# Cross-attention on one core: softmax denominators by transposed sums on VectorE instead of matrix products with ones

## The reference, cut to what matters

```
a = layer_norm(ctx) * gamma + beta                  # (32, 375, 512)
Q = x @ Wq.T;  K = a @ Wk.T;  V = a @ Wv.T          # 16 heads of 32
attn = softmax(where(mask, Q K^T * 32**-0.5, -inf)) # over the 375 context rows
out = x + tanh(gate) * ((attn @ V) @ Wo.T)
```

## Time and profile before

| | |
|---|---|
| median of 3 runs | 940.44 us |
| the profiled execution, whole | 940.45 us |
| its span, first to last instruction | 938.4 us |
| PE busy | 928.2 us (99%) |
| DVE, ACT, POOL busy | 706.4, 685.8, 639.4 us |
| L1123, 992 records in the loop | 35.1 us busy, 259 ns each |
| L870, L873, L876, 31 each | 645, 241, 645 ns each |
| L855, 384 records | 625 ns each |
| L680, 62 records | 543 ns each |

### The profile page before, as it was taken

One profiled execution on the slowest core, in us unless ns is written; L12 is line 12 of the kernel. 1 busy time (PEld: TensorE's weight loads), 2 busy tenths in 40 slices (PEclk: granted clock), 3 DMA queues, 4 the chain that ended last, 5 costly groups with the idle time before them and its releaser, 6 DMA issues.

```text
span 938.4 us, 26747 instructions
## 1 busy us (share of the span) xinstructions
PE 928.2 (99%) x10723; PEld 805.9 (86%) x10723; DVE 706.4 (75%) x1381; ACT 685.8 (73%) x1296; POOL 639.4 (68%) x724
## 2 busy tenths in 40 slices
PE   9999999999999999999999999999999999999997
PEld 8898888888888888888888888888888888888885
DVE  6972498778777778777877777877787777887677
ACT  3422687777778787787877778777787777878775
POOL 0672366777777777777777777877777777777765
PEclk9999999999999999999999999999999999999999
DMA  9983143334344433444434443344443443334212
GB/s 280 344 266 150 29 101 93 92 104 115 90 98 113 111 92 88 104 113 116 105 85 111 115 107 82 93 111 114 115 98 90 113 114 95 91 94 113 56 39 59
DMA packets 85850, 105.54 MB, mean 112 GB/s; under 512 B 22528, under 2 KB 63488, under 8 KB 85728
## 3 DMA queue, kind: packets, MB, share of 16 engines
q1 hardware_dynamic: 85152, 102.93, 41.3%
q10 hardware_dynamic: 576, 0.92, 0.3%
HBM read 86.39 MB, written 17.43 MB: 111 GB/s over the span
## 4 chain that ended last, share of the span: by engine, by line
PE 95%; DMA 1%; DVE 1%; ACT 1%; SPq 0%; issue 0%; DVEq 0%
PE banks L959 66%; PE banks L1104 10%; PE banks L1117 8%; PE banks L982 7%; PE banks L1123 2%; DMA shared_f<-in_xT 1%; ACT shared_q L630 0%; ACT shared_q L639 0%; DMA x_odd<-row_stats 0%; DVE shared_q L865 0%; PE banks L1085 0%; DVE shared_r L751 0%; PE banks L990 0%; SPq L319 0%; ACT shared_f L644 0%
## 5 line engine op out<-in xcount | busy, mean ns | idle before, releaser
L959 PE MATMUL banks<-shared_r,w_k 128*128 128x376 f32 x1536 | 291.7, 339 | 0.6 <-ACT shared_f L680 0.5
L630 ACT ACTIVATE shared_q<-banks,maskT,rstd 125x448 f32<-125x448 f32 x384 | 243.4, 729 | 55.3 <-PE banks L1104 55.0
L959 PE MATMUL banks<-w_v,shared_r 128*125 128x512 f32 x1152 | 283.5, 395 | 0.0
L855 DVE TRANSPOSE_TENSOR_REDUCE rmax<-shared_q 128x14 f32<-128x448 f32 x384 | 219.8, 625 | 82.3 <-ACT shared_q L630 81.1
L959 PEld LDWEIGHTS banks<-shared_r,w_k 128*128 128x128 f32 x1536 | 263.1, 188 | 13.5 <-issue 0.9
L493 POOL TENSOR_TENSOR shared_f<-shared_q 125x448 f32<-125x448 f32 x124 | 142.0, 1145 | 163.7 <-PE banks L1123 163.2
L959 PEld LDWEIGHTS banks<-w_v,shared_r 128*125 128x125 f32 x1152 | 212.9, 186 | 44.5
L865 DVE TENSOR_TENSOR shared_q<-shared_q,banks 125x448 f32<-125x448 f32 x384 | 208.2, 607 | 0.1
L639 ACT ACTIVATE shared_q<-shared_q 125x448 f32<-125x448 f32 x384 | 186.4, 568 | 2.5 <-DVE shared_q L865 2.5
L497 POOL TENSOR_TENSOR shared_f<-shared_f,shared_q 125x448 f32<-125x448 f32 x124 | 142.3, 1148 | 9.7
L461 POOL TENSOR_TENSOR shared_r<-cn,shared_r 128x375 fp32r<-128x375 f32 x124 | 112.3, 927 | 42.9 <-ACT shared_r L591 42.8
(11 more groups left out here) (93 smaller groups left out, 785.1 us busy)
## 6 DMA issues: line engine op xcount, KB each, us to landing
cn<-in_ctxT SPq DMA_DIRECT2D x128, 187.5 KB, 4.0
rows<-in_ctx SPq DMA_DIRECT2D x32, 720.0 KB
xy<-in_x SPq DMA_DIRECT2D x32, 224.0 KB, 7.4
q_kept<-shared_q SPq DMA_DIRECT2D x8, 896.0 KB, 7.5
shared_q<-q_kept SPq DMA_DIRECT2D x32, 224.0 KB, 3.9
out<-xy SPq DMA_DIRECT2D x32, 224.0 KB, 3.8
shared_f<-in_xT SPq DMA_DIRECT2D x7, 896.0 KB, 11.3
x<-row_stats SPq DMA_DIRECT2D x64, 84.0 KB
```

The source lines that it names most:

```text
L630: act.activation(prob[0:SP_, n % NB, j, :] .rearrange("p (a h t) -> p a h t", a=2, h=2), score_view(n, j), ACT.Identity, bias=maskT[0:SP_, ...
L855: last = dve.tensor_reduce(rmax[:, n % 2, BLK * j:BLK * j + BLK], prob[:, n % NB, j, :].rearrange("p (k a) -> p k a", a=32), AX.X, ALU.max ...
L959: last = pe.matmul(dst, l, m, start=(start and k == 0), stop=(stop and k == len(pairs) - 1))
```

## The change

For batches 0 to 28 (SUMMED = B - 3 = 29, so slots p < 116) TensorE's products with ones are gone. VectorE takes a transposed sum of each `psum` half (`partial_sums`: one value per query and quadrant into `parts`). Once per batch SyncE stores these to DRAM and loads them so that the four quadrants lie side by side on 32 partitions (`store_parts`, `load_parts`); VectorE adds the four, takes the reciprocal and transposes (`shares`); SyncE stores the result and loads it back spread over all 128 partitions in four loads (`store_shares`, `load_shares`) into `rshare`. GpSimd multiplies with that one batch step later: `normalised(c-3)`, `add_bias(c-3)` and `low_half(c-3)` now all stand in the even slot pair, and ScalarE's `high_half(c-3)` in the middle of it. Batches 29 and 30 keep the way of before, and 31 the one that it has in the last steps. `psum`'s rows 96 to 127 are set to zero once, since the transposed sum reads all 128. GpSimd's `sum_chunks` waits for VectorE's sum of the buffer instead of TensorE's product.

```diff
+        SUMMED = B - 3
             for m in range(PAIRS):
                 c, odd = divmod(m, 2)
+                if summed(c - 2):
+                    if odd:
+                        store_shares(c - 2)
+                    else:
+                        store_parts(c - 2)
                 store_maxima(2 * m)
                 store_maxima(2 * m + 1)
                 load_maxima(2 * m)
                 load_maxima(2 * m + 1)
+                if summed(c - 2):
+                    if odd:
+                        load_shares(c - 2)
+                    else:
+                        load_parts(c - 2)
...
             def normalised(b):
-                pool.wait_ge(rspread_done, b + 1)
                 o = pv[:, b % 2 * HT:b % 2 * HT + HT]
-                pool.tensor_tensor(o, o, rspread[:, :], ALU.mult).then_inc(o_norm, 1)
+                if b < SUMMED:
+                    pool.wait_ge(ld_shares, 64 * b + 64)
+                    pool.wait_ge(pv_out, b * KT + KT)
+                    pool.tensor_tensor(o, o, rshare[:, :], ALU.mult).then_inc(o_norm, 1)
+                else:
+                    pool.wait_ge(rspread_done, b - SUMMED + 1)
+                    pool.tensor_tensor(o, o, rspread[:, :], ALU.mult).then_inc(o_norm, 1)
...
-                need(pool, pv_mm, p - 1)
+                if p - 2 < SUMMED * KT:
+                    need(pool, part_done, p - 1)
+                else:
+                    pool.wait_ge(pv_mm, p - 1)
...
-                if odd and 1 < c < B - 1:
-                    low_half(c - 2)
                 if not odd and m >= 0:
-                    if c > 1:
-                        normalised(c - 2)
+                    if c > 2:
+                        normalised(c - 3)
+                        add_bias(c - 3)
+                        low_half(c - 3)
+                    if m == PAIRS - 2:
+                        normalised(B - 3)
                     if c + 1 < B and c > 0:
                         row_statistics(c + 1)
-                    if c > 2:
-                        add_bias(c - 3)
...
+                if p < SUMMED * KT:
+                    act.wait_ge(sum_done, p + 2)
+                    at = p % 8 * T
+                    act.activation(pv[:, at:at + 2 * T], bank[b][:, 0:2 * T], ACT.Copy) \
+                        .then_inc(pv_out, 2)
+                    return
...
+            def partial_sums(p):
+                dve.wait_ge(sum_done, p + 1)
+                if p % KT == 0:
+                    need(dve, parts_stored, p // KT * 16)
+                u = p % KT
+                dve.tensor_reduce(parts[:, BLK * u:BLK * u + BLK],
+                                  psum[:, p % 2, :].rearrange("p (k a) -> p k a", a=32),
+                                  AX.X, ALU.add, apply_transpose=True).then_inc(part_done, 1)
+
+            def shares(b):
+                dve.wait_ge(ld_parts, 16 * b + 16)
+                n = KT * BLK
+                dve.tensor_reduce(whole_sum[:, 0:n], part4[:, :].rearrange("p (q k) -> p k q", q=HC),
+                                  AX.X, ALU.add).then_inc(whole_done, 1)
+                dve.wait_ge(whole_done, b + 1)
+                dve.reciprocal(whole_sum[:, 0:n], whole_sum[:, 0:n]).then_inc(share_step, 1)
+                dve.wait_ge(share_step, b + 2)
+                need(dve, shares_stored, 16 * b)
+                dve.transpose(share_rows[:, :], whole_sum[:, :]).then_inc(share_done, 1)
...
-                if not odd and c > 1:
-                    normalise(c - 2)
+                if m == PAIRS - 2:
+                    normalise(B - 3)
...
+                for p in (2 * m - 4, 2 * m - 3):
+                    if 0 <= p < SUMMED * KT:
+                        partial_sums(p)
+                if not odd and 0 <= c - 2 < SUMMED:
+                    shares(c - 2)
...
+                if p < SUMMED * KT:
+                    last.then_inc(pv_mm, 2)
+                    return
                 for q in range(2):
                     pe.wait_ge(sum_done, p + q + 1)
                     denominator(psum[:, q, :], to[:, (2 + q) * T:(3 + q) * T], True, True) \
```

More of the change, by code:

```diff
@@ L544, in _ @@
                 pool.memset(prob[96:128, q, :, :], LOWEST).then_inc(low_done, 1)
-            pool.wait_ge(low_done, NB)
             pool.wait_ge(q_out, GROUPS * KT)
+            for q in range(2):
+                pool.memset(psum[96:128, q, :], 0.0).then_inc(low_done, 1)
+            pool.wait_ge(low_done, NB + 2)
             pool.wait_ge(c_done, KT)
@@ L705, in slot_pair @@
                     second_out(m)
-                if odd and 1 < c < B - 1:
-                    high_half(c - 2)
                 if pair(m - 3):
@@ L715, in slot_pair @@
                     k_out(2 * m + 2)
+                if not odd and c > 2:
+                    high_half(c - 3)
+                if pair(m + 1):
                     first_out(m + 1)
@@ L808, in centre @@
                         .then_inc(centred[w], 1)
+            dve.memset(whole_sum[:, :], 1.0).then_inc(share_step, 1)
             x_group(1)
```

59 lines of the change are left out of this document (51 added, 8 removed).

## The result

The changed kernel takes 979.95 us, the median of 4 runs (976.49 to 983.3), beside 940.6 us for the kernel before on the same chip (4 runs). The ratio is 1.0417, 95% interval 1.038 to 1.0455. I had forecast 922.4 us: it is 57.6 us slower than that, and on the other side of the kernel before.

What follows compares the result with a forecast made beforehand. TensorE, busy 99% and alone in the steady chain, was taken as the bound. Span 938.4 - 22.3 (denominators) - 0.3 (ScalarE copy) + 4.6 (tail) = 920.4, plus 2.05 outside it: 922.4 us, range 916.5 to 931.

Steps and rivals of the forecast that it cites:

- Step 1: TensorE: the denominator matmuls go in 58 slot pairs at 0.385 us each, saving 22.3 us (bounds 22.0 and 28.4).
- Step 2: VectorE: loses normalise, gains transposed sums and three small instructions; occupied 22.3 of 25.4 us per batch, so costs nothing.
- That round trip: Parts through DRAM: load issued at T = 7.6 behind x_odd, landed at 11.2 (bounds 9.6, 11.6); VectorE stands about 1.2 us.
- Step 3: GpSimd's additions and later normalising, and share loads on SP: low_half ready with 1.0 us slack, shares in time, no cost.
- Cost nothing: GpSimd's later normalising and low_half: slack 1.0 us before the output product, 1.6 us for the normalising by itself.
- rule for lateness: VectorE in the odd slot pair: 2 us of lateness is covered; every further microsecond is paid once per batch.
- Rival (c): VectorE becomes the bound through slow transposed ADD: overruns from 1.4 us each, at 1.6 us 948 us; chance 0.04.
- (a): Shares land late every batch; 0.3 us past T = 3.95 costs 8.4 us over 28 batches: 930.8 us; chance 0.12.
- (b): Share loads run one after the other, 7.4 us too late, 207 us: about 1130 us; chance 0.07 for anything over 942.
- Step 4: ScalarE: its copy of the weighted sums halves to 224 columns, saving 0.3 us (bounds 0 and 0.5).
- Step 5: Tail, slot pair 63: TensorE stands 4.6 us once for low_half (bounds 3.3, 5.8); normalise(29), 4.3 us late, hides in this stall.
- Rival (d): TensorE's clock falls in the tail's 4.6 us stall: 2 us more, 924.5 us; chance 0.15.

Runs made afterwards that it cites:

- experiment 1: Kernel before, without TensorE's products with ones in slots 0 to 115 and nothing in their place (denominators set to 1): 918.87 us in one run.
- experiment 5: Changed kernel with the four share loads behind the odd slot pair's prefetches on SyncE's queue instead of ahead of them: 1013.27 us in one run.
- Experiment 9: Changed kernel with the rows loads issued earlier on SyncE's queue, at the end of the even slot pair: 926.01 us, ratio 0.9847.
- experiment 2: Changed kernel with two parts buffers, shares(b) reading those of batch b-1, so nobody waits for this batch's part load: 929.05 us in one run.
- experiment 11: Changed kernel, rows loads on ScalarE's queue, batch 31's third V product in slot pair 63, batch 28's output product behind the loop: 926.34 us, ratio 0.9844.

## Why the prediction was wrong

**Step 1** held: 22.3 us forecast (bounds 22.0 to 28.4), 21.0 measured in one run (experiment 1), a slot pair of 12.70 us as forecast.

**Step 2** is where it failed, in the paragraph "That round trip". I put the issue of the part load at T = 7.6, right behind x_odd at T = 7.0, both read from the kernel before, and its landing at 11.2 (bounds 9.6 to 11.6). That is what the first batch shows, and nearly the last; in the 27 between it was issued at T = 9.6 to 12.0 (11.1 in the batch shown, 478.73 less 467.60) and in at 13.1 to 15.3, on average 14.2. The error is in the issue; from issue to landing it took 3.7 us where I had 3.6. I carried the moment of x_odd over from a schedule in which the stores ahead of it meet no traffic. I had looked at the DMA share behind the issue of x_odd, 0.22, and not at where the odd slot pair's burst ends, about 0.5 us ahead of the stores on which x and x_odd wait.

**Step 3** saw the other half and drew nothing from it: "Behind them on SP stand only loads used a slot pair or more later; the seven new issues per batch are 7 x 0.53 = 3.7 us of SP's 25.4." Nobody waits for these loads, true, but they are 1.3 MB, and what is issued next are the even slot pair's maxima stores. I costed a delayed transfer by its own reader, not by what it collides with; and the later odd maxima of Step 2 (VectorE 1.1 us late in the odd slot pair, by my own count) I had not followed to SyncE either. That the shares themselves land in time held, and experiment 5 shows how thin it is. "Cost nothing" for GpSimd did not quite hold: the late exponentials, for which its additions wait (138.7 us, 29 times), make the low half late by 0.2 us in 20 batches, 3.9 us. Experiment 9, without the collision, has one such wait beside the tail's.

Step 2's rule for lateness (a cover of 2 us, each further microsecond paid once a batch) had its cover right and its price too low. In the batch shown the subtractions end at odd T = 13.3 (494.06 less 480.74), where I had 10.0, and the scores stand 1.48 us, from 11.9 on: a cover of 1.9. With the average landing, 14.2 instead of 11.2, the rule gives 27 x 1.0 = 27 us; TensorE stood 18.3 us on subtractions in all. What it leaves out is what comes with that stall. TensorE's span is 60.5 us longer than in experiment 1 (977.5 and 917.0). Idle time makes up 36.2 us of it: 18.3 on subtractions, 9.6 on ScalarE's copy and 8.3 on the low half, 4.4 of these the tail's. The rest is a longer busy time, 930.9 and 906.0, that is 24.9 us (0.6 too much in the sum): about 9 us of them are the six K products at the lower clock (3.4 to 3.9 us instead of 2.3), 2.5 us the output product of the tail, and about 6 us scores that the stall cuts in two (0.70 and 1.14 us instead of 1.51, 19 times). Some 7 us are not traced row by row.

VectorE's small instructions cost 0.55 + 0.49 + 0.23 = 1.27 us where I took 1.0; two transposed sums take 1.15 to 1.17 us, at the lower end of my 0.55 to 0.65 each. **Rival (c)**, VectorE as the bound, is refuted by experiment 2, although the sign that I had tied to it, an idle before the scores on a subtraction, appeared: that sign says that VectorE is late, not why. **Rivals (a) and (b)**, late share loads, did not occur (no wait on them in the changed kernel's list), but the collision is of their kind, at a transfer I had not suspected.

**Step 4**, 0.3 us for ScalarE, is too small to be told in any run here. **Step 5** held for the stall: 4.6 us forecast, 4.37 measured. Its bracket on normalise(29) was right too, as experiment 11 shows, and hid that removing one wait is worth nothing without the other. **Rival (d)** came in where I gave it 0.15: the stall cost 2.5 us more at half clock. My price of 2 us came near by luck, for it was taken from the first 4.21 us of matmuls, where the trace gives the granted clock as 1.00. The page "TensorE: Matmul & The Clock Gate" of the Trainium skill, under "Why this matters for your kernels", had warned of such gaps, and the rows bear it out.

With the collision gone, the forecast fits: experiment 9 has 926.0. To 922.4 add 1.65 us (its output product takes 4.60 instead of 2.95) and 1.3 us (21.0 instead of 22.3), and 0.7 us is left.

## What to carry to other kernels

A new small transfer on the path has to be placed against the bursts that are in flight when it is issued, and a new issue on a queue against what it pushes back: ask not only who reads the delayed load, but which short store or load is issued next, and read the DMA share in windows up to that moment. Here a 1.3 MB burst was moved by some 2 us of issue time and 3.5 us of a later VectorE, and a forecast gain of 18 us became a loss of 39; issuing 750 KB of the same loads at another moment turned that into a gain of 14. Read such a distance in several batches, and measure it from the same event in both kernels: the batch first looked at had the longest issue of all. A stretch that behaves as forecast once (here the first batch) and not after it points to a circle, in which a late wait makes the next one later. When a stall in the tail is removed, follow every engine that waits for the same event.

## What the runs showed of the hardware

- A store of 21 KB is in at most 1.6 us after its issue when the DMA engines are idle (462.41 to 464.01; their share was 0.00 to 0.17 from 461 to 464). Behind 1.3 MB of prefetches, with a DMA share of 0.7 to 1.0, the load that waits for the first of two such stores went out 5.1 us after the second was issued, not 0.1. Putting the burst on another engine's queue changes nothing in that: 2.66 us with the rows from ScalarE's queue, 2.74 from SyncE's.
- TensorE's clock fell to its lower level not only behind the 4.37 us stall (0.50, 5.46 us for 2.95 us of work) but also in the steady part, in six batches, behind an idle of 1.18 to 1.90 us before 1.14 us of scores and mostly one of 0.38 us behind them (0.51 from 495.6 to 497.6). It did not behind 0.89 us or less, nor in two batches behind 1.15 and 1.21 us. In the batch shown the idle of 1.48 us cost 1.55 us more (3.85 less 2.30).
